# A transformer kernel on one core: the inverse roots of its normalizations in eight small VectorE operations in place of eleven, and double roots in one chain

## The reference

```python
def _layernorm(x, axis=-1, eps=1e-05):
    m = jnp.mean(x, axis=axis, keepdims=True)
    v = jnp.var(x, axis=axis, keepdims=True)
    return (x - m) / jnp.sqrt(v + eps)
...
x = x + 0.5 * _L2_ffn_ref(_layernorm(x, axis=-1), ...)
x = x + _L2_attn_ref(_layernorm(x, axis=-1), ...)
```

## Time and profile before

| | us |
|---|---|
| median of three runs | 2247.57 (2246.85 to 2248.11) |
| the profiled execution, its own time | 2253.42 |
| its span | 2251.7 |
| busy in it: PE | 2030.9 (90%) |
| PE weight loads | 1265.8 (56%) |
| DVE | 1493.1 (66%) |
| ACT | 1003.9 (45%) |
| POOL | 263.3 (12%) |

### The profile page before, as it was taken

The page is one execution under the profiler, slowest core; times in us unless marked ns, Lnnn a source line. Parts: engine busy times, 40 slices in busy tenths (PEclk is TensorE's granted clock), DMA queues, the critical chain, the costliest instruction groups (busy, mean ns, idle before and its releaser), DMA issues.

```text
span 2251.7 us, 39009 instructions
## 1 busy us (share of the span) xinstructions
PE 2030.9 (90%) x13210; PEld 1265.8 (56%) x13224; DVE 1493.1 (66%) x4290; ACT 1003.9 (45%) x1879; POOL 263.3 (12%) x408
## 2 busy tenths in 40 slices
PE   7999999998959799999999998868898899998898
PEld 3423333325638556666666665657574567775576
DVE  6779999966526556666666664535656645877786
ACT  4257777773314255555555553225332333442133
POOL 2261111110054200000000000244000000000000
PEclk9989999998979999999999999979998999999999
DMA  6200000000126300000000000236200000000000
GB/s 225 62 33 28 23 26 27 25 8 22 41 66 196 104 1 1 1 0 0 0 0 0 0 1 15 76 99 200 78 1 0 1 1 1 1 1 1 1 1 19
DMA packets 62913, 78.10 MB, mean 35 GB/s; under 512 B 18954, under 2 KB 36637, under 8 KB 62016
## 3 DMA queue, kind: packets, MB, share of 16 engines
q1 hardware_dynamic: 57536, 67.18, 9.7%
q0 software_dynamic: 4672, 8.99, 1.6%
q10 hardware_dynamic: 576, 0.26, 0.1%
HBM read 64.14 MB, written 10.88 MB: 33 GB/s over the span
## 4 chain that ended last, share of the span: by engine, by line
PE 77%; DVE 9%; ACT 4%; issue 4%; another core or an unknown queue 3%; DMA 1%; SPq 1%; DVEq 0%; ACTq 0%; POOL 0%; POOLq 0%
PE ps L451 12%; PE ps L433 12%; PE ps L1061 6%; PE ps L2556 5%; PE ps L1027 5%; PE ps L2519 5%; PE ps L2540 5%; PE ps L1044 4%; PE ps L829 3%; PE ps L840 2%; PE ps L1011 2%; PE ps L1993 2%; DVE x L1245 1%; ACT arena L1164 1%
## 5 line engine op out<-in xcount | busy, mean ns | idle before, releaser
L451 PEld LDWEIGHTS ps<-l_w,arena 128*128 128x128 f32 x2560 | 343.3, 196 | 221.3 <-issue 157.9
L451 PE MATMUL ps<-l_w,arena 128*128 128x128 f32 x2560 | 348.0, 280 | 56.9 <-ACT arena L502 44.4
L2806 DVE TENSOR_REDUCE arena<-ps 128x1 f32<-128x512 f32 x512 | 326.1, 685 | 40.1 <-PE ps L2519 40.1
L433 PE MATMUL ps<-xnT,l_w 128*128 128x512 f32 x640 | 341.5, 618 | 3.0 <-ACT xnT L265 3.0
L582 DVE SCALAR_TENSOR_TENSOR x<-ps,comb,x 128x128 f32<-128x128 f32 x576 | 162.2, 345 | 206.0 <-PE ps L451 137.7
L2711 ACT ACTIVATE arena<-ps 128x1024 f32<-128x1024 f32 x256 | 252.6, 1022 | 102.3 <-PE ps L2540 101.7
L1227 DVE TENSOR_REDUCE arena<-ps 128x1 f32<-128x128 f32 (+7 forms) x256 | 178.8, 751 | 159.9 <-PE ps L1033 159.9
L502 ACT ACTIVATE arena<-ps,l_b 128x512 f32<-128x512 f32 x192 | 131.5, 687 | 283.4 <-PE ps L433 217.0
L1172 ACT ACTIVATE arena<-ps 128x512 f32<-128x512 f32 (+1 forms) x192 | 85.5, 489 | 252.1 <-PE ps L1044 251.8
L1164 ACT ACTIVATE arena<-ps,arena 128x128 f32<-128x128 f32 (+7 forms) x256 | 187.0, 745 | 13.3 <-DVE arena L1227 13.3
L2519 PE MATMUL ps<-arena 72*128 72x512 bf16 x512 | 184.5, 389 | 1.6 <-DVE arena L2806 1.1
(11 more groups left out here) (446 smaller groups left out, 2725.6 us busy)
## 6 DMA issues: line engine op xcount, KB each, us to landing
arena<-in_l_w SPq DMA_DIRECT2D x124, 256.0 KB
l_w<-in_l_w SPq DMA_DIRECT2D x2, 2048.0 KB, 14.3
l_w<-in_l_w SPq DMA_DIRECT2D x4, 1024.0 KB, 12.4
arena<-s_parts_q SPq DMA_DIRECT2D x28, 144.0 KB
arena<-s_parts_k SPq DMA_DIRECT2D x28, 144.0 KB
arena<-l_y_rows SPq DMA_DIRECT2D x12, 256.0 KB
s_parts_q<-arena SPq DMA_DIRECT2D x6, 256.0 KB, 3.3
s_parts_k<-arena SPq DMA_DIRECT2D x2, 768.0 KB, 4.8
```

What stands on the lines that cost most here:

```text
L433: pe.matmul(k.ps[:, n % 2, :], w.w1[:, e, f * P:(f + 1) * P], k.xnT[:, g * GW:(g + 1) * GW], start=True, stop=True).then_inc(s.hidden_mm.s ...
L451: ins = pe.matmul(k.ps[:, 2 + e % 4, j * P:(j + 1) * P], w.h[:, n % 2, j * P:(j + 1) * P], w.w2[:, e, f, :], start=(f == 0 and j == 0), st ...
L2806: dve.tensor_reduce(s.nm2[:, place, qt, half:half + 1], k.ps[:, bank, :], AX.X, ALU.max, negate=True)\
```

## The change

`rsqrt` has eight instructions in place of eleven. The first guess is one instruction (the integer value of the number times -0.5 plus a constant, L119) in place of two; then one corrected Newton step of three instructions (L120 to L122), with constants that fit the first guess, and one step of higher order with four (L123 to L126). All eight are still waited for one by one. In `front_stats` with `inner=True` the second root no longer depends on the first: the argument of r1 and that of r1 r2 are written side by side (L239, L240, the first without a wait of its own), and one chain of eight instructions works on both, each instruction on two rows of four numbers. The rows of `k.small` that hold the results are the same as before (3 and 7), so `front_rows` is unchanged. `row_stats` gets the closed form too, though no call of it uses `inner`. No line of PE, ACT, POOL or SP changes, nor the numbers of filler matmuls.

```diff
--- before.py
+++ after.py
@@ -21,6 +21,7 @@
 GW = GT * P
 NE = 8
 EPS = 1e-5
+FIRST_ROOT = 0.703952253
 
 
 class Steps:
@@ -115,12 +116,14 @@
 
 def rsqrt(dve, st, v, y, t):
 
-    st.done(dve.tensor_scalar(t.bitcast(I32), v.bitcast(I32), 1, None, ALU.logical_shift_right))
-    st.done(dve.tensor_scalar(y.bitcast(I32), t.bitcast(I32), -1.0, float(0x5F3759DF), ALU.mult, ALU.add))
-    for _ in range(3):
-        st.done(dve.scalar_tensor_tensor(t, y, -0.5, y, ALU.mult, ALU.mult))
-        st.done(dve.tensor_tensor(t, t, v, ALU.mult))
-        st.done(dve.scalar_tensor_tensor(y, t, 1.5, y, ALU.add, ALU.mult))
+    st.done(dve.tensor_scalar(y.bitcast(I32), v.bitcast(I32), -0.5, float(0x5F1FFFF9), ALU.mult, ALU.add))
+    st.done(dve.scalar_tensor_tensor(t, y, -FIRST_ROOT, y, ALU.mult, ALU.mult))
+    st.done(dve.tensor_tensor(t, t, v, ALU.mult))
+    st.done(dve.scalar_tensor_tensor(y, t, FIRST_ROOT * 2.38924456, y, ALU.add, ALU.mult))
+    st.done(dve.scalar_tensor_tensor(t, y, 0.375 ** 0.5, y, ALU.mult, ALU.mult))
+    st.done(dve.tensor_tensor(t, t, v, ALU.mult))
+    st.done(dve.scalar_tensor_tensor(t, t, -1.25 / 0.375 ** 0.5, t, ALU.add, ALU.mult))
+    st.done(dve.scalar_tensor_tensor(y, t, 1.875, y, ALU.add, ALU.mult))
 
 
 def token_stats(dve, k, g):
@@ -140,7 +143,7 @@
         for i in range(n):
             last = dve.bn_stats(stat[:, i, :], src[:, i, :])
         st.done(last)
-    mean, rstd, d, v, t, v2, r2 = (sm[:, k, 0:n] for k in range(7))
+    mean, rstd, d, v, t, v2 = (sm[:, k, 0:n] for k in range(6))
     me, mo = stat[:, 0:n, 1], stat[:, 0:n, 4]
     se, so = stat[:, 0:n, 2], stat[:, 0:n, 5]
     dve.tensor_tensor(mean, me, mo, ALU.add)
@@ -150,14 +153,11 @@
     dve.tensor_scalar(v, v, 1.0 / width, None, ALU.mult)
     st.done(dve.scalar_tensor_tensor(d, d, 0.25, d, ALU.mult, ALU.mult))
     st.done(dve.tensor_tensor(v, v, d, ALU.add))
-    st.done(dve.tensor_scalar(v2, v, EPS, None, ALU.add))
+    if inner:
+        st.done(dve.tensor_scalar(v2, v, 1.0 + EPS, EPS * EPS, ALU.mult, ALU.add))
+    else:
+        st.done(dve.tensor_scalar(v2, v, EPS, None, ALU.add))
     rsqrt(dve, st, v2, rstd, t)
-    if inner:
-        st.done(dve.tensor_tensor(d, rstd, rstd, ALU.mult))
-        st.done(dve.tensor_tensor(v, v, d, ALU.mult))
-        st.done(dve.tensor_scalar(v2, v, EPS, None, ALU.add))
-        rsqrt(dve, st, v2, r2, t)
-        st.done(dve.tensor_tensor(rstd, rstd, r2, ALU.mult))
     return mean, rstd
 
 
@@ -230,15 +230,15 @@
     for t in range(lo, hi):
         ins = dve.bn_aggr(sm[:, 0:2, t], k.stat[:, t, :])
     st.done(ins)
-    mean, var, v, rstd, t, w, r2, both = (sm[:, i, lo:hi] for i in range(8))
-    st.done(dve.tensor_scalar(v, var, EPS, None, ALU.add))
-    rsqrt(dve, st, v, rstd, t)
-    if inner:
-        st.done(dve.tensor_tensor(w, rstd, rstd, ALU.mult))
-        st.done(dve.tensor_tensor(w, w, var, ALU.mult))
-        st.done(dve.tensor_scalar(v, w, EPS, None, ALU.add))
-        rsqrt(dve, st, v, r2, t)
-        st.done(dve.tensor_tensor(both, rstd, r2, ALU.mult))
+    if not inner:
+        var, v, rstd, t = (sm[:, i, lo:hi] for i in range(1, 5))
+        st.done(dve.tensor_scalar(v, var, EPS, None, ALU.add))
+        rsqrt(dve, st, v, rstd, t)
+    else:
+        t, v, rstd = (sm[:, i:i + 5:4, lo:hi] for i in range(1, 4))
+        dve.tensor_scalar(v[:, 0], t[:, 0], EPS, None, ALU.add)
+        st.done(dve.tensor_scalar(v[:, 1], t[:, 0], 1.0 + EPS, EPS * EPS, ALU.mult, ALU.add))
+        rsqrt(dve, st, v, rstd, t)
 
 
 def front_rows(dve, k, norm, g, inner=False, plain=None):
```

## The result

| | before | changed |
|---|---|---|
| median | 2247.84 us (4 runs, 2246.85 to 2248.27) | 2224.85 us (4 runs, 2220.94 to 2231.48) |
| ratio, 95% interval | | 0.9903 [0.9879, 0.9927] |
| profiled execution, span | 2253.42, 2251.7 | 2220.94, 2219.2 |
| mean granted clock | 0.958 | 0.968 |

The change is 23.0 us faster by the medians, where 16.1 us were forecast. The profiled pair lies 32.5 us apart; single executions spread by some 10 us, so only part of that belongs to the change.

What follows compares the result with a forecast made beforehand. PE, busy 90% of the span, bounds the kernel; DVE counts only where PE waits. Single roots 6.65, double roots 3.44 and 3.26, clock 2.75: 16.1 us off 2247.57 gives 2231.5 us, range 2226 to 2238 (8 in 10).

Steps and rivals of the forecast that it cites:

- The price of a step: Each waited DVE instruction in a root costs the distance between starts, 0.1985 us at 4 columns, 0.21 at 16.
- Rival 4: Overlap: removed instructions cost only their issue, 0.08 us each, 67 of them 5.4 us; 2242.2 us, chance 0.02.
- rival 5: The new instructions are slower, 0.275 us each, so single roots give nothing; about 2242 us, chance 0.02.
- The waits: PE's wait at the second group falls from 8.24 to about 4.8 us, single places by 0.6, the last group's vanishes.
- The clock at the last group: Twelve projections behind the last group's wait return to full clock, 5.39 us in place of 8.14; 2.75 us won.
- Rival 1: The clock stays low at the last group, everything else as forecast; 2234.2 us, chance 0.22.
- behind the long ones the clock stays low as before: At the other ten waits idle time shrinks by 0.6 us; no clock gain was counted there.
- rival 2: The clock is kept at more places, among waits of 1.87, 2.22 and 1.23 us; 2228 us, chance 0.16.
- Rival 3: Only the double roots pay, 6.7 us; at single roots PE returns earlier into 1.2 GHz or other waits; 2240.9, chance 0.08.
- the eleven single roots: Single roots on the path, whose end PE waits for, directly or through ACT; 0.56 to 0.63 us each, sum 6.65 us.
- Rival 6: Slower: the clock falls more often, one more low stretch at seven of thirteen places costing 19.3 us; 2253.5, chance 0.01.
- The hidden roots: 18 single roots and two middle groups' double ones, covered by filler, PE's own work or a gather DMA; counted as nothing.

Runs made afterwards that it cites:

- dummy steps: Changed kernel with three waited dummy instructions ahead of each single root and 17 ahead of each inner one, restoring the old step counts; ratio 1.0000 against the kernel before.
- the kernel with one chain: Kernel before with only the inner (double) roots merged into one chain, every root still of eleven steps; ratio 0.9963, 8.3 us less.

## Why the prediction was right, and where its size was off

- **The price of a step** held: 8 and 10 rows where 11 and 27 stood, 0.20 us each at all shapes, and with as many dummy steps the gain is nothing. Rival 4 (overlap, 0.08 us) and rival 5 (slower instructions) fall by the timeline. The Trainium skill (VectorE: DVE Perf Modes, the section on the TRN2 errata) itself says, below the row of 58 cycles that I had set against the 0.20 us and named at rival 4, that this row under-predicts and that the measured fixed term is about 150 cycles. With 4 columns I estimate 0.160 us from that, and the traces' 0.16 to 0.17 us agree.
- **The waits** shrank as forecast: 8.24 to 4.77, the last group's to nothing, five others by 0.59 to 0.63. ACT's copy ended the next wait at the last group (3.46 us for 3.26).
- **The clock at the last group** came back and was worth 8.14 - 5.39 = 2.75 us. Rival 1 falls.
- **The step that failed** is the sentence "behind the long ones the clock stays low as before", and the nothing that I counted for the clock at the other ten waits. With the shorter waits the full clock stayed at layer 2's second mixture (1.6 us each time, the one place that all thirteen traces bear out), and came back sooner at the second group (1.5 us in all three traces of the changed kernel, but also in one of the five with the full wait, and by 0.9 us in another). In some executions it was also kept in the retention and behind the start of the second time-mixing layer (0.7 us each on the mean); there the clock comes out either way, and that the change is the cause isn't shown. That is rival 2, to which I gave 0.16, at one of the places that it named (2.22 us) and at others that it didn't; its 2228 is nearest to the 2224 to 2228 of three comparisons. The other two of its places gave no clock: at 1.23 us there was none to win (the stretch lost exactly 0.60), and at 1.87 us the clock behind it came out either way in both kernels.
- **Rival 3** falls by the eleven single roots alone, 9.7 us. **Rival 6** (slower) needed five places with more of the low clock. There is one: from the root at 2108.9 us to the next it took 11.70 us before, and 12.84 and 12.67 in two of three traces of the changed kernel; the stretch that holds it is shorter all the same.
- **The hidden roots** gave nothing in the part that traces can compare.
- **The range** of 2226 to 2238 ended 1.15 us above the first median. I had given its lower end half of 2.75 us at two waits; the traces have 2.7 to 5.9 us in the last third alone. The mechanism of the 16.1 us held; the term that was too small is the clock's.

Left open: the first two thirds of the program. There one of two durations shows in layer 0's attention, 445.7 to 445.9 us in three traces and 440.2 to 441.3 in ten. The three all have the eleven steps ahead of it, but three others that have them too show 441.1 to 441.3, so whether the change makes the shorter one likelier isn't shown. It, and the gathers, are why the profiled pair lay 32.5 us apart: without any edit in that part, the kernel with one chain reached layer 1's block 22 in 1539.1 us, against 1548.8.

## What to carry to other kernels

A chain of small waited DVE operations costs its count times the distance between starts, whatever the few columns; take steps out only of chains whose end PE waits for, and merge chains that don't need one another. Where PE waits, price the clock at every wait that gets shorter, the long ones too, not only at the one that vanishes: the same 0.6 us was worth 0.6 us at one place and 2.2 at another by what stood behind it. A trace is one execution: before reading a few us of clock into a change, look how far two traces of one kernel differ there. And where a wait can't be shortened, a few filler matmuls in it, ending about a microsecond ahead of the data, gave 10 us on top of the change and 16 us without it.

## What the runs showed of the hardware that I had not expected

**One chip is 62 to 65 us faster than two others on the same kernel** (2184.12 us against 2249.55 and 2246.37), and nearly all of it lies in the two sparse mixtures. PE's timeline in the first, of the kernel before:
```profile
646.35 2.08 PE L451 MATMUL ps<-l_w,arena 128*128 128x128 f32 x8 [5.09 <-issue]
...
663.17 2.07 PE L451 MATMUL ps<-l_w,arena 128*128 128x128 f32 x8 [13.04 <-ACT arena L502]
...
674.45 2.08 PE L451 MATMUL ps<-l_w,arena 128*128 128x128 f32 x8 [7.50 <-ACT arena L502]
```
and the same place in its trace on the faster chip:
```profile
639.69 1.05 PE L451 MATMUL ps<-l_w,arena 128*128 128x128 f32 x8
640.58 1.02 PE L433 MATMUL ps<-xnT,l_w 128*128 128x512 f32 x2
```
While the gathers run, ACT's activation comes out late, three times here, and the profile has no more for what released it than another core or an unknown queue; why the chips differ stays open; from root to root the stretch takes 164.4 and 133.4 us, and that in the second mixture 165.9 and 133.0. Every version shares it, so it doesn't touch the comparison, but a time of this kernel means nothing without before beside it on the same chip.

**The same idle time can leave either clock.** In the retention PE is idle 0.60 and, behind four transposes, 2.95 us; the work behind it ran partly at 1.2 GHz in two of three traces of the changed kernel and at the full clock in the third. At the dummy steps' last group and second group, above, the full clock came back sooner behind waits that were as long as before. The Trainium skill (TensorE: Matmul & The Clock Gate, "HAM oscillation — how this bites in real kernels") describes work between waits that starts at the low clock again and again. The traces agree in that the low clock returns at wait after wait; behind ones as short as 2.2 us it did so too, though the transposes right behind them (0.66 us) still ran at the full clock.
